# Half of each tile's weighed edge slots are added to the other half by an adding DMA before the segment sums

## What is computed

```python
w_m = (efeat @ W_msg + b_msg).reshape(E, 16, 16)
w_a = (efeat @ W_attn + b_attn).reshape(E, 16, 16)
h_src = feat[src][:, :, None]
e1 = w_m * h_src
e2 = w_a * h_src
seg_max = segment_max(e2, dst)
ex = exp(e2 - seg_max[dst])
denom = segment_sum(ex, dst)
ft = segment_sum(e1 * (ex / denom[dst]), dst)
x = layernorm(x + ft.sum(axis=1))
```

## Time and profile before

| | |
|---|---|
| median of three runs | 1732.97 us (1730.08 to 1733.81) |
| the profiled execution | 1732.84 us, its span 1731.0 us |
| VectorE busy | 1537.4 us, 89% of the span |
| TensorE busy | 1354.0 us, 78% |
| GpSimd busy | 974.1 us, 56% |
| ScalarE busy | 889.1 us, 51% |
| moved by DMA | 182.94 MB, mean 106 GB/s |
| TensorE's granted clock | 0.962 of full speed over the span |

### The profile page before, as it was taken

One profiled execution on the slowest core, in us unless ns is written; L12 is line 12 of the kernel. 1 busy time (PEld: TensorE's weight loads), 2 busy tenths in 40 slices (PEclk: granted clock), 3 DMA queues, 4 the chain that ended last, 5 costly groups with the idle time before them and its releaser, 6 DMA issues. The chain is left out here.

```text
span 1731.0 us, 20720 instructions
## 1 busy us (share of the span) xinstructions
PE 1354.0 (78%) x5767; PEld 690.3 (40%) x5767; DVE 1537.4 (89%) x1614; ACT 889.1 (51%) x1842; POOL 974.1 (56%) x878
## 2 busy tenths in 40 slices
PE   0002899999999999999999999999999999998400
PEld 0001444444444444444444444444444444444200
DVE  8534899999999999999999999999999999998458
ACT  1002566666666666666666666666665555554100
POOL 5777777777676676776777676676661000000170
PEclk9999899999999999999999999999999999999655
DMA  4314344444444444444444444444443222221150
GB/s 109 76 19 112 93 122 117 125 122 117 126 119 116 127 119 117 127 118 116 128 118 117 127 118 117 127 118 118 126 116 105 94 81 80 95 71 54 56 147 18
DMA packets 174990, 182.94 MB, mean 106 GB/s; under 512 B 47056, under 2 KB 130328, under 8 KB 174878
## 3 DMA queue, kind: packets, MB, share of 16 engines
q1 hardware_dynamic: 140958, 158.74, 29.1%
q0 software_dynamic: 33920, 22.89, 8.3%
HBM read 92.36 MB, written 89.41 MB: 105 GB/s over the span
## 5 line engine op out<-in xcount | busy, mean ns | idle before, releaser
L488 POOL DMA_INDIRECT split<-x_parts,edge_src x784 | 880.6, 1123 | 351.3 <-issue 220.1
L781 PE MATMUL bank_sum<-em,row_onehot 128*128 128x512 f32 x1760 | 891.4, 609 | 31.3 <-ACT sum_rows L647 31.0
L1024 DVE TENSOR_TENSOR em<-bank_prod,h_rows 128x1024 f32<-128x1024 f32 x440 | 524.2, 1212 | 64.1 <-PE bank_prod L769 58.1
L781 PEld LDWEIGHTS bank_sum<-em,row_onehot 128*128 128x128 f32 x1760 | 299.0, 189 | 222.8 <-issue 184.1
L1042 DVE TENSOR_TENSOR em<-em 128x1024 f32<-128x1024 f32 x220 | 267.7, 1217 | 3.5 <-ACT em L606 3.5
L769 PE MATMUL bank_prod<-w_rows,partsT 100*128 100x512 bf16 x880 | 269.3, 388 | 1.0 <-DMA partsT<-tile_table 0.6
L647 ACT COPY sum_rows<-bank_sum 128x512 f32<-128x512 f32 x220 | 126.8, 576 | 275.6 <-PE bank_sum L781 254.6
L1067 DVE TENSOR_TENSOR em<-em,bank_max 128x2048 f32<-128x2048 f32 x110 | 250.7, 2279 | 3.2 <-ACT node_max L638 3.2
L606 ACT ACTIVATE em<-em 128x2048 f32<-128x2048 f32 x110 | 210.5, 1914 | 3.6 <-DVE em L1067 3.6
L630 ACT COPY chunk_fwd<-bank_max 128x512 f32<-128x512 f32 x110 | 64.5, 586 | 276.7 <-PE bank_max L712 276.7
L769 PEld LDWEIGHTS bank_prod<-w_rows,partsT 100*128 100x128 bf16 x880 | 86.7, 99 | 249.2 <-issue 203.1
(11 more groups left out here) (165 smaller groups left out, 1171.0 us busy)
## 6 DMA issues: line engine op xcount, KB each, us to landing
sums<-sum_rows SPq DMA_DIRECT2D x110, 512.0 KB
rec<-split_records SPq DMA_DIRECT2D x220, 144.0 KB, 2.2
split_records<-split SPq DMA_DIRECT2D x97, 288.0 KB, 2.1
mask<-tile_table SPq DMA_DIRECT2D x110, 192.0 KB, 3.2
split<-x_parts,edge_src POOLq DMA_INDIRECT x784
rel<-tile_table SPq DMA_DIRECT2D x110, 64.0 KB, 3.0
edge_feat<-in_features SPq DMA_DIRECT2D x97, 64.0 KB
flag<-tile_table SPq DMA_DIRECT2D x110, 2.0 KB
```

The costliest lines, as they stand in the source:

```text
L488: return nc.gpsimd.indirect_dma_start(out, None, src, bass.IndirectOffsetOnAxis(idx, 0))
L781: mm = nc.tensor.matmul(bank_sum[:, :], row_onehot[:, t % RING, g, :], em[:, t % RING, s * GROUPS + g, :, :, :].rearrange("p i m o -> p (i ...
L1024: V.tensor_tensor(em[:, v, 2 * j:2 * j + 2, :, :, :].rearrange("p s i m o -> p s i (m o)"), bank_prod[j % 2][:, :, :].rearrange("p s (i x) ...
```

## The change

The layout of `em` changes: a tile is now [2 halves, 2 sides, 4 pieces, 256 values]. A half h holds slots 2h and 2h+1 of both groups; the side m is attention or message, and the 256 values of a side are contiguous. The weights, the constants and the reads of the results are reordered to match, and `h_rows` holds each feature row twice. The ring of `em` has five tiles in place of four (`EM_RING`); some small tables of the first and last part move into its space.

GpSimd, after it has waited for both `weigh` steps of tile t, issues one DMA with `accum_op=ALU.add`, SBUF to SBUF: half 1 of the tile (2,048 fp32 values for each of 128 partitions, 1 MB) is added to half 0. Its place is between the seventh and the eighth gather of set t+11 (it is issued for tile t-1 in iteration t, which gathers set t+10). `sum_slots` waits for that DMA and multiplies half 0 alone: two pieces for each group in place of four. Its calls stand at new places in TensorE's order, the first one behind `give_features(t+2)`. ScalarE does `copy_parts(t+2)` ahead of `exponents(t-1)`.

```diff
@@ GpSimd
-            for q in range(PREP_FIRST, PREPS):
-                gather_features(q)
+            def gather_some(q, edges):
+                if not prep(q):
+                    return
+                u, n = q % PREP_RING, prep_rows(q)
+                if edges[0] == 0:
+                    pool.wait_ge(in_landed[u], 32 * (q // PREP_RING + 1))
+                for e in edges:
+                    at = H_AT + H_WORDS * (e % SLOTS)
+                    gather(split[0:n, u, e // SLOTS, at:at + H_WORDS], xs_d,
+                           edge_src[0:n, u, e:e + 1]).then_inc(h_landed[u], 16)
+
+            def add_halves(t):
+                if not tile(t):
+                    return
+                pool.wait_ge(weighted, 2 * (t + 1))
+                e = em[:, t % EM_RING, :, :, :, :].rearrange("p h m k x -> p h (m k x)")
+                nc.gpsimd.dma_start(e[:, 0, :], e[:, 1, :], accum_op=ALU.add).then_inc(added[t % 2], 16)
+
+            for t in range(FIRST, LAST + 1):
+                gather_some(t + LEAD, range(0, 7))
+                add_halves(t - 1)
+                gather_some(t + LEAD, range(7, 8))
@@ ScalarE
-                nc.scalar.copy(h_rows[:, t % 2, :, :].rearrange("p g k -> p (g k)"),
-                               bank_t[0][:, 0:GROUPS * SLOTS * FEAT]).then_inc(h_copied, 1)
+                rows = bank_t[0][:, 0:GROUPS * SLOTS * FEAT].rearrange("p (y k) -> p y k", k=FEAT)
+                nc.scalar.copy(h_rows[:, t % 2, :, :, :, :].rearrange("p g s m k -> p (g s) m k"),
+                               bc(rows, 2, [P, GROUPS * SLOTS, 2, FEAT])).then_inc(h_copied, 1)
...
+                copy_parts(t + 2)
                 exponents(t - 1)
-                copy_parts(t + 2)
@@ TensorE
-            def sum_slots(t, g, slots):
+            def sum_slots(t, g, pair):
                 if not tile(t):
                     return
-                if slots[0] == 0:
-                    pe.wait_ge(weighted, 2 * (t + 1))
+                if pair == 0:
+                    pe.wait_ge(added[t % 2], rounds(t, 2))
                     pe.wait_ge(onehot_ready, 2 * (t + 1))
                     since(pe, sums_copied, 2 * t + g)
-                for s in slots:
-                    mm = nc.tensor.matmul(bank_sum[:, :], row_onehot[:, t % RING, g, :],
-                                          em[:, t % RING, s * GROUPS + g, :, :, :].rearrange("p i m o -> p (i m o)"),
-                                          start=(s == 0), stop=(s == SLOTS - 1))
+                mm = nc.tensor.matmul(bank_sum[:, :].rearrange("p (m x) -> p m x", m=2), row_onehot[:, t % RING, g, :],
+                                      em[:, t % EM_RING, 0, :, pair * GROUPS + g, :], start=(pair == 0), stop=(pair == 1))
...
                 turn_maxima(t)
                 give_parts(t + 2)
-                sum_slots(t - 2, 0, [0])
                 products(t + 1, 2)
                 give_features(t + 2)
-                sum_slots(t - 2, 0, [1])
+                sum_slots(t - 2, 0, 0)
                 products(t + 1, 3)
-                sum_slots(t - 2, 0, [2])
+                sum_slots(t - 2, 0, 1)
                 turn_back(t)
-                sum_slots(t - 2, 0, [3])
                 products(t + 2, 0)
+                sum_slots(t - 2, 1, 0)
                 pick_ends(t)
-                sum_slots(t - 2, 1, [0])
                 products(t + 2, 1)
-                sum_slots(t - 2, 1, [1, 2, 3])
+                sum_slots(t - 2, 1, 1)
@@ VectorE
-                    since(v_eng, sums_ready, 2 * (t - RING + 1))
+                    since(v_eng, sums_ready, 2 * (t - EM_RING + 1))
...
-                m = em[:, t % RING, 4 * half:4 * half + 4, :, 1, :]
-                V.tensor_tensor(m, m, em[:, t % RING, 4 * half:4 * half + 4, :, 0, :], ALU.mult).then_inc(weighted, 1)
+                e = em[:, t % EM_RING, half, :, :, :].rearrange("p m k x -> p m (k x)")
+                V.tensor_tensor(e[:, 1, :], e[:, 1, :], e[:, 0, :], ALU.mult).then_inc(weighted, 1)
```

More of the change, by code:

```diff
@@ L64 @@
 RING = 4
+EM_RING = 5
+HALF = SIDE // 2
 OUT_RING = 3
@@ L168, in gnn_kernel @@
         flag4 = sb("flag4", [SLOTS, 2, WIDE], BF16)
-        h_rows = sb("h_rows", [P, 2, GROUPS, SLOTS * FEAT])
+        h_rows = sb("h_rows", [P, 2, GROUPS, SLOTS, 2, FEAT])
         partsT = sb("partsT", [KROWS, 2, SIDE * P], BF16)
-        em = sb("em", [P, RING, SIDE, FEAT, 2, FEAT])
-        max4 = sb("max4", [P, 4, FEAT, FEAT])
+        em = sb("em", [P, EM_RING, 2, 2, HALF, ATT])
+        max4 = sb("max4", [P, HALF, ATT])
         chunk_max = sb("chunk_max", [P, 2, GROUPS * ATT])
@@ L213, in region @@
             return em_flat[:, at:at + k * width].rearrange("p (k r) -> p k r", k=k)
+        spare = em[0:TILES, EM_RING - 1, :, :, :, :].rearrange("p h m k x -> p (h m k x)")
+        table = spare[:, 0:COLUMNS * WIDE].rearrange("p (j c) -> p j c", c=COLUMNS)
+        filled = spare[:, COLUMNS * WIDE:2 * COLUMNS * WIDE].rearrange("p (c j) -> p c j", c=COLUMNS)
+        c_a, c_b, c_first, c_end = [spare[:, (2 * COLUMNS + k) * WIDE:(2 * COLUMNS + k + 1) * WIDE] for k in range(4)]
         r_rows = region(0, 4, BOTH)
@@ L223, in gnn_kernel @@
         fin = region(0, NODE_COLS, BOTH)
+        f_sum, f_mid = [region(NODE_COLS * BOTH + a * NODE_COLS * FEAT, NODE_COLS, FEAT) for a in range(2)]
+        out_rows = em_flat[:, NODE_COLS * (BOTH + 2 * FEAT):NODE_COLS * (BOTH + 3 * FEAT)]
         iotas = sem("iotas")
@@ L286, in gnn_kernel @@
         shifted = sem("shifted")
+        added = [sem(f"added{u}") for u in range(2)]
         exp_done = sem("exp_done")
@@ L1020, in times_features @@
                     v_eng.wait_ge(h_copied, t + 1)
-                    since(v_eng, sums_ready, 2 * (t - RING + 1))
+                    since(v_eng, sums_ready, 2 * (t - EM_RING + 1))
                 v_eng.wait_ge(prod_ready, 4 * t + j + 1)
-                h = h_rows[:, t % 2, :, FEAT * j:FEAT * (j + 1)]
-                V.tensor_tensor(em[:, v, 2 * j:2 * j + 2, :, :, :].rearrange("p s i m o -> p s i (m o)"),
-                                bank_prod[j % 2][:, :, :].rearrange("p s (i x) -> p s i x", i=FEAT),
-                                bc(h, 3, [P, GROUPS, FEAT, 2 * FEAT]), ALU.mult).then_inc(times_h, 1)
+                k = 2 * (j % 2)
+                h = h_rows[:, t % 2, :, j, :, :]
+                V.tensor_tensor(em[:, t % EM_RING, j // 2, :, k:k + 2, :].rearrange("p m k (i o) -> p k m i o", o=FEAT),
+                                bank_prod[j % 2][:, :, :].rearrange("p k (m i o) -> p k m i o", m=2, o=FEAT),
+                                bc(h, 4, [P, GROUPS, 2, FEAT, FEAT]),
+                                ALU.mult).then_inc(times_h, 1)
             def run_forward(t):
@@ L1064, in shift @@
                 v_eng.wait_ge(max_copied, t + 1)
-                e = em[:, t % RING, :, :, 0, :].rearrange("p (s g) i o -> p s (g i) o", g=GROUPS)
-                m = bank_max[:, :].rearrange("p (x o) -> p x o", o=FEAT)
-                V.tensor_tensor(e, e, bc(m, 1, [P, SLOTS, GROUPS * FEAT, FEAT]), ALU.subtract).then_inc(shifted, 1)
+                e = em[:, t % EM_RING, :, 0, :, :].rearrange("p h (s g) x -> p h s (g x)", g=GROUPS)
+                m = bank_max[:, :].unsqueeze(1).unsqueeze(1).to_broadcast([P, 2, 2, GROUPS * ATT])
+                V.tensor_tensor(e, e, m, ALU.subtract).then_inc(shifted, 1)
             for t in range(FIRST, LAST + 1):
@@ L1121, in _ @@
                 v_eng.wait_ge(r_turned, 4 * c + 4)
-                V.tensor_copy(r_back[0:TILES, c, :].rearrange("p (i m o) -> p m i o", m=2, o=FEAT),
-                              bank_prod[c // 2][0:TILES, c % 2, :].rearrange("p (m i o) -> p m i o", m=2, i=FEAT)
-                              ).then_inc(r_placed, 1)
+                V.tensor_copy(r_back[0:TILES, c, :], bank_prod[c // 2][0:TILES, c % 2, :]).then_inc(r_placed, 1)
             def sums_of(c, m):
-                return fin[0:NODE_P, 5 * c:5 * c + 5, :].rearrange("p n (i m o) -> p n i m o", m=2, o=FEAT)[:, :, :, m, :]
+                return fin[0:NODE_P, 5 * c:5 * c + 5, m * ATT:(m + 1) * ATT]
             for c in range(5):
```

38 lines of the change are left out of this document (12 added, 26 removed).

## The result

The changed kernel takes **2160.3 us** (median of 4 runs, 2153.7 to 2164.6) against 1733.0 for the kernel before on the same chip: a ratio of **1.2466 [1.2426, 1.2506]**, 427 us slower. The forecast was 2090 us. The profiled run took 2164.6 us with a span of 2162.8; the mean granted clock fell from 0.96 to 0.81. Of the run with the small add, further down, one of four executions took 2791 us where the others took 1911 to 1924, and it is left out of that ratio.

A forecast was written before the change was run, and what follows sets the result against it. DVE was taken to lead with PE close behind, and the wait for the adding DMA to bind after the change. 88 tiles x 3.5 us plus 20 x 2.5 gave 358 us on 1733: 2090 us, range 1670 to 2350.

The forecast's parts named there:

- The removed work: Sum matmuls on PE (L781): half of the 16 for each tile go, 4.1 us of PE in each tile.
- the ceiling: Most that could be won with DVE at its busy time, 12.6 us an iteration in the loop: 59 us in all.
- The layout at nothing: DVE's steps in the loop on the new `em` layout: same element counts, so 0 cost for all layout edits.
- ScalarE's order at nothing: `copy_parts` ahead of `exponents`: PE reaches the first sum at about 810.4 in place of 811.36; no gain priced.
- L: Time from the end of a tile's weighing to the landing of its adding DMA: 10.2 us, 9.2 in the last 20 tiles.
- two reads, no company: Case for the adding DMA's landing: both halves are read and no other transfers share the engines, 8.5 us.
- The data part: The adding DMA's bytes: 2.1 MB in and 1.05 MB out at 385 GB/s, 5.4 us.
- The fixed part: The adding DMA's time apart from bytes: 2.6 us from issue to landing plus 0.5 for a delayed issue, 3.1 us.
- The company: Other transfers on the DMA engines beside the add: some 3.5 us of overlap at full; the middle between none and full taken.
- The loop L + 6.3: Weighing, adding DMA, sum pair, product, DVE, next weighing: an iteration can't be shorter than L + 6.3 us; 16.5 forecast.
- The rival: Add below half the copy rate, or PE's clock halved: an 18.1 to 19.9 us iteration, up to 2480 us; above 2350, chance 0.16.
- The end of the loop: Last weighing, lone DMA, matmuls and copy after the last tile: ends at 1613.7 against 1613.5, nothing gained.

The follow-up runs named there:

- the run with the small add: The changed kernel with its adding DMA cut to 16 of 2,048 values of a partition, issue and waits kept; 1921.5 us, ratio 1.1079.
- B undone: The changed kernel with the flags of tile t+3 loaded ahead of the store of the split records on SyncE's queue; 2009.6 us, ratio 1.1612.
- B and C undone: The changed kernel with the flags loaded ahead of the split records' store and `pick_ends` ahead of the first sum of group 1; 1979.3 us, ratio 1.1445.
- the copy: The kernel with B and C undone, with a plain DMA copy of half 1 over half 0 in place of the add; 1799.6 us, ratio 1.0391.
- With the bytes away: The changed kernel adding only 16 of 2,048 values of a partition, with `pick_ends` ahead of the first sum of group 1; 1754.1 us, ratio 1.0131.
- With the other waits away: The kernel with B and C undone, with sums, their copies and stores moved from tile t-2 to tile t-3; 1736.2 us, ratio 1.0031.

## Why the prediction was right in size and only half right in mechanism

**The removed work and the ceiling.** 880 sum matmuls as counted, and an iteration without waits takes 12.44 us, against 12.6 foreseen. But no run holds it while gathers run: the shortest mean there is 12.80 us, in the version without the add and with the flags first. A ceiling set by DVE alone left out GpSimd.

**The layout at nothing.** Right: L1045, L1064 and L1087 take 1.212, 1.216 and 2.287 us, and the kernel without the add isn't slowed by it.

**ScalarE's order at nothing.** Wrong. The prediction said that it lets PE start earlier and then gave it no price; it is worth 25 us. In the kernel with only this swap the iterations take 12.74 us on the mean of the loop, before 12.99; DVE waits for products in 18 tiles of the stretch of the earlier trace rows, before in nearly every one; the 18 are longer, 23.3 us in all against 29.7, and PE stands 25.4 us for late flags in them. The prediction had put the end of the short waits down to the removed matmuls, as part of its ceiling of 59 us; this swap alone ends them. The changed kernel has the swap too; without it, it might well be slower still, but that wasn't run.

**GpSimd.** Right for the changed kernel: the issue took 0.944 us on the mean against 1.0 to 1.2, and GpSimd rests some 6 us in each tile. The gathers are 969 ns on the mean, against the 1.141 us of the earlier trace rows. But the prediction took a gather's time as given, and so found 1.4 us to spare. In the versions without the long waits a gather takes 1.22 to 1.30 us on the mean, and GpSimd has nothing to spare; by the prediction's own sign, "GpSimd is never idle in the loop", the queue of issues sets the pace there.

**L.** The term was mis-sized: 10.2 us taken, 7.8 measured in the turn shown above, 0.3 us to the issue and 7.5 from issue to landing (the medians are 7.3 with B undone and 7.5 with B and C undone). That is below the 8.5 of "two reads, no company", and below the 8 to 12 us that the prediction named as its sign. The data part was right: 5.4 us by two reads at 385 GB/s, and 5.4 is what the add takes beyond the small add. The fixed part was 3.1 us and is 0.3 + 2.1 = 2.4. The company was the larger error, 1.7 us taken: in the loop the add lands after 7.5 us and almost alone after 7.2 to 7.5. The prediction let the other transfers slow the add; in the trace the add slows them. "Collectives: The Full Stack" of the Trainium skill says of a reduce, in the section on the bandwidth ceiling, that the second source halves the rate; the trace agrees (5.4 us against 2.6 for the copy, above). The formula of 2.0 us plus the bytes over 436 GB/s in "DMA: Bandwidth & Descriptors", in the section on the anatomy of a DMA on the SWDGE path, gives an estimate of 4.4 us for this transfer; the copy, at 4.66 us, is near it, but 6.9 us was the shortest measured for the add, and the measurement decides.

**The loop L + 6.3.** Real, but in the changed kernel mostly hidden behind other waits. With the measured L it gives 14.1 us an iteration at the full clock; with the prediction's L it gave 16.5, and 16.87 were measured. So the right size was partly luck: it came from a term too large in place of two that were missing:

- *What the add delays.* The missing question is who waits for the small transfers beside a large one. The 2 KB of flags, issued behind the store, land after up to 4.4 us and more, and `give_features`, the sums and the products are queued behind them on PE. Putting them first gives 151 us back. Of what slows them the runs show only that it needs the bytes (0.2 us of such waits with the small add).
- *The moved sums.* The diff puts `sum_slots(t - 2, 1, 0)` ahead of `pick_ends`; the prediction doesn't name this, and so has it at nothing without a reason. But group 1 uses the same bank as group 0 and waits for ScalarE's copy, 2.0 us a tile, and the shift waits behind it 2.4. With the bytes away it is 167 us; with the bytes there and the flags first, 30.

**The clock.** The rival had 0.16, with a price for a clock that is halved all through. It came in partly: 0.79 between 800 and 1000 us, where the kernel before had the full clock. A sum pair then takes 2.04 to 2.08 us in place of 1.12, and each wait on PE becomes longer for it: 1.3 us an iteration in the version with B and C undone. With the other waits away the mean of the loop is 13.1 us, and 12.85 without the three iterations of 20 to 28 us; against the 12.44 of an undisturbed iteration that leaves 0.4 us, 108 x 0.4 = 43 us as an estimate, which the clock shares with a full GpSimd. Only the last 20 tiles measure it alone, at 0.44 us an iteration.

**The end of the loop.** The last 14 iterations take 15.3 us (15.5 foreseen), but most of their waits are before the shift and for ScalarE's copy, not for the add. The last add, almost alone, takes 7.2 us from issue to PE, against 8.5. The prediction's time for the end is wrong as a sum: 1599.95 + 8.5 + 2.0 + 0.6 is 1611.1, not 1613.7. From the end of the last weighing to the end of the last copy it is 16.5 us, where it was 13.6, as each group's four matmuls take 3.8 us at the lower clock.

## What to carry to other kernels

Before a large transfer goes into a loop, list the small transfers that are queued behind or beside it and ask what the engines wait for: such a wait costs as much as one for the large transfer, and issuing the small one first cost nothing here. Price a matmul group that is moved ahead of another by what it waits for, its bank's copy above all, and by everything queued behind it. When a change brings several waits at once, each stands behind another: undone alone, one of them gained nothing and was worth 167 us later, so undo them together before one is dismissed, and give a transfer that is truly late a whole iteration more (243 us here). Before work is moved off an engine, look at who is next: here DVE needed 12.44 us an iteration and GpSimd 12.84, of 12.97 in all, so relieving PE could win little.

## What was not expected of the hardware

- An adding DMA of 1 MB between two places of SBUF lands 6.9 / 7.3 / 8.5 us (least, median, most) after its issue in the run with the flags first, and 7.5 on the median where the loop waits for it in every tile. It writes in bursts of up to 524 GB/s with empty slices of 0.25 us between; beside the copy of as many bytes the slices show 212 to 459. The same add of 64 bytes for each partition lands after 2.1 us.
- Its issue holds GpSimd for 0.96 us, that of the copy for 0.57.
- A gather that GpSimd runs beside DVE's weighing lasted 4.33 us in the turn shown, where others take 0.94; on the mean of a loop a gather takes from 0.96 to 1.30 us.
- A 2 KB load issued on SyncE beside it takes 0.98 us to issue on the median, where the same instruction takes 0.32 in the runs with the small add.
- TensorE's granted clock can change from one iteration to the next (1.00 in one, 0.66 in the next), between levels of 2.4 and 1.2 GHz, when the engine waits a few us in each: here matmul pairs of 1.12 and 2.08 us stand side by side.
